# Part sums of finished accumulators spread over four units, and GpSimd's values made one group ahead, in a four-layer graph attention network

## What is computed

```python
h = x @ W                                   # per head
e = leaky_relu(s_src[i] + s_dst[j])         # slope 0.01 or 0.2
alpha = softmax(where(adj, e, -inf), axis=j)
out = alpha @ h                             # layer 0: then elu
```

## Time and profile before

| what | value |
| --- | --- |
| time, median of 3 runs | 3360.18 us (3354.19 to 3361.27) |
| time of the profiled execution | 3357.18 us |
| its span | 3355.4 us |
| busy, PE / DVE / ACT / POOL | 3011.8 / 2278.4 / 1914.1 / 1226.3 us |
| mean granted clock of PE | 0.961 |

### The profile page before, as it was taken

The page is one execution under the profiler, slowest core; times in us unless marked ns, Lnnn a source line. Parts: engine busy times, 40 slices in busy tenths (PEclk is TensorE's granted clock), DMA queues, the critical chain, the costliest instruction groups (busy, mean ns, idle before and its releaser), DMA issues.

```text
span 3355.4 us, 74122 instructions
## 1 busy us (share of the span) xinstructions
PE 3011.8 (90%) x26664; PEld 2751.1 (82%) x26664; DVE 2278.4 (68%) x4091; ACT 1914.1 (57%) x3380; POOL 1226.3 (37%) x1640
## 2 busy tenths in 40 slices
PE   6588899999955999999997999999999998569997
PEld 5587899999945999999995787887887886359997
DVE  4888788887777888888776555655655554454447
ACT  4455798889845898898884454444454443320000
POOL 2433456551214555545212013223223232324443
PEclk9799999999987999999998999999999998789999
DMA  7465000000100000000010000000000000000001
GB/s 258 177 243 205 10 13 11 12 13 13 61 0 11 13 13 11 12 13 10 12 40 7 9 2 4 4 1 4 4 1 4 1 1 2 0 1 0 0 0 50
DMA packets 42286, 104.58 MB, mean 31 GB/s; under 512 B 9904, under 2 KB 23472, under 8 KB 33968
## 3 DMA queue, kind: packets, MB, share of 16 engines
q1 hardware_dynamic: 42160, 102.92, 9.1%
HBM read 98.51 MB, written 4.39 MB: 31 GB/s over the span
## 4 chain that ended last, share of the span: by engine, by line
PE 73%; DVE 15%; issue 5%; DMA 3%; POOL 2%; ACT 1%; DVEq 1%; SPq 0%; POOLq 0%; ACTq 0%
PE bank L970 16%; PE bank L967 16%; PE bank L1014 14%; PE bank L1052 11%; PE bank L973 10%; DVE sums L1454 4%; DVE rings L1509 3%; PE bank L931 2%; DMA arena<-in_adj_dram 2%; DVE rings L1512 2%; PE bank L1041 2%; PE bank L1028 1%; PE bank L945 1%; DVE rings L1503 1%; DVE arena L1212 1%
## 5 line engine op out<-in xcount | busy, mean ns | idle before, releaser
L967 PE MATMUL bank<-values,rings 128*128 128x195 bf16 x8192 | 1418.4, 247 | 138.0 <-DVE rings L1512 79.0
L760 ACT ACTIVATE above<-srow,kpass 128x512 fp8e4<-128x512 f32 x2048 | 1292.9, 709 | 294.3 <-DVE rings L1512 278.6
L970 PE MATMUL bank<-values,rings 128*128 128x195 bf16 x8192 | 1418.6, 249 | 0.0
L967 PEld LDWEIGHTS bank<-values,rings 128*128 128x128 fp8e4 x8192 | 809.2, 99 | 157.2 <-issue 155.8
L970 PEld LDWEIGHTS bank<-values,rings 128*128 128x128 fp8e4 x8192 | 787.1, 96 | 1.1
L1509 DVE TENSOR_TENSOR rings<-rings,above 128x512 uint32<-128x512 uint32 x512 | 385.1, 752 | 237.2 <-PE bank L970 190.5
L778 ACT ACTIVATE values<-srow,cmul 128x512 f32<-128x512 f32 x256 | 205.9, 814 | 433.3 <-PE bank L1052 432.3
L1052 PE MATMUL bank<-hv,values 128*128 128x257 f32 x1792 | 423.8, 382 | 9.5 <-DVE values L1388 9.5
L1512 DVE TENSOR_TENSOR rings<-rings 128x512 uint32<-128x512 uint32 x512 | 408.6, 798 | 17.5
L1052 PEld LDWEIGHTS bank<-hv,values 128*128 128x128 f32 x1792 | 336.9, 191 | 80.5 <-issue 25.5
L973 PE MATMUL bank<-values,rings 128*128 128x195 bf16 x4096 | 349.3, 248 | 23.0 <-DVE rings L1500 23.0
(11 more groups left out here) (177 smaller groups left out, 3505.4 us busy)
## 6 DMA issues: line engine op xcount, KB each, us to landing
arena<-in_adj_dram SPq DMA_DIRECT2D x64, 1024.0 KB, 5.7
srow<-src_dram SPq DMA_DIRECT2D x72, 256.0 KB, 3.2
x<-in_x_dram SPq DMA_DIRECT2D x1, 4096.0 KB, 14.3
out_dram<-x SPq DMA_DIRECT2D x8, 512.0 KB, 2.9
arena<-in_L_gnn_fe_w_dram SPq DMA_DIRECT2D x2, 512.0 KB, 10.0
arena<-in_L_gnn_W_hz_dram SPq DMA_DIRECT2D x1, 1024.0 KB, 10.4
arena<-in_L_gnn_g_w_dram SPq DMA_DIRECT2D x1, 1024.0 KB, 11.6
weights<-in_L_gnn_W_dram SPq DMA_DIRECT2D x3, 256.0 KB, 3.3
```

The source lines that it names most:

```text
L760: last = act.activation(above[:, k % 2, q, :], srow[:, par, :], ACT.Relu, scale=BIG, bias=kpass[:, slot, q * BITS + k:q * BITS + k + 1], s ...
L967: pe.matmul(acc[:, 0:KW], pos[:, k % 2, q, :].bitcast(FP8)[:, rows], v[:, 0:KW], start=first, stop=final, skip_group_check=True)
L970: last = pe.matmul(acc[:, KW:2 * KW], neg[:, k % 2, q, :].bitcast(FP8)[:, rows], v[:, KW:2 * KW], start=False, stop=final, skip_group_chec ...
```

## The change

In layers 0 and 1, from the second pass of layer 0 on, the four part sums of a finished group are made one each in the units 1, 2, 3 and 4 of the group that follows, after the exclusive-or; the wait for banks and quotient stands ahead of the first, and `s_sums` is signalled by the last. The first pass of layer 0 (`at_once`) and layer 3 keep all four at once. On POOL, in every pass that makes values (three passes in each of layers 0, 1 and 3), the values of group 0 are made ahead of the loop, each trip makes the values of group g + 1 before the quotient of group g, and the last values and the last two quotients stand behind a loop of three double trips.

```diff
@@ -586,16 +586,33 @@
                     if p < H - 1:
 
                         pool.wait_ge(s_unit, p * UNITS + (CREDIT + TURN[l] * H * UNITS))
-                    with pool.Fori(0, NG // 2) as gg:
+                    if p == H - 1:
+                        with pool.Fori(0, NG // 2) as gg:
+                            for par in range(2):
+                                g = gg * 2 + par
+                                chain.enter(g, links)
+                                quotient(l, p, g, par)
+                        chain.leave(NG)
+                        continue
+
+                    def next_values(g):
+                        for kind in range(kinds):
+                            made = value_parts(pool, chain, vtmp_pool, kind, g * GT, GT, p + 1, 1 - p % 2)
+                        made.then_inc(s_vals, 1)
+
+                    next_values(0)
+                    chain.settle()
+                    with pool.Fori(0, NG // 2 - 1) as gg:
                         for par in range(2):
                             g = gg * 2 + par
                             chain.enter(g, links)
-                            if p < H - 1:
-                                for kind in range(kinds):
-                                    made = value_parts(pool, chain, vtmp_pool, kind, g * GT, GT, p + 1, 1 - p % 2)
-                                made.then_inc(s_vals, 1)
+                            next_values(g + 1)
                             quotient(l, p, g, par)
-                    chain.leave(NG)
+                    chain.leave(NG - 2)
+                    next_values(NG - 1)
+                    quotient(l, p, NG - 2, 0)
+                    quotient(l, p, NG - 1, 1)
+                    chain.settle()
                 if l < 3:
                     return
 
@@ -1442,16 +1459,23 @@
                 chain.leave(FIRST_CHUNKS)
                 rest_of_first_values(l)
 
+            def sum_parts(l, half, slot, it):
+
+                kinds = 2 if l < 3 else 1
+                parts = bank[GT * half + it][:, 0:kinds * KW].rearrange("p (k a c) -> p k c a", k=kinds, a=PARTS)
+                return dve.tensor_reduce(sums[:, slot, it, 0:kinds, :], parts, AX.X, ALU.add)
+
+            def banks_ready(l, count):
+
+                dve.wait_ge(s_unit, count * BITS + (TURN[l] * H * UNITS + CREDIT))
+
+                dve.wait_ge(s_quot, count + (TURN[l] * H * NG + CREDIT - 1))
+
             def evacuate(l, half, slot, count):
 
-                kinds = 2 if l < 3 else 1
-
-                dve.wait_ge(s_unit, count * BITS + (TURN[l] * H * UNITS + CREDIT))
-
-                dve.wait_ge(s_quot, count + (TURN[l] * H * NG + CREDIT - 1))
+                banks_ready(l, count)
                 for it in range(GT):
-                    parts = bank[GT * half + it][:, 0:kinds * KW].rearrange("p (k a c) -> p k c a", k=kinds, a=PARTS)
-                    last = dve.tensor_reduce(sums[:, slot, it, 0:kinds, :], parts, AX.X, ALU.add)
+                    last = sum_parts(l, half, slot, it)
                 last.then_inc(s_sums, 1)
 
             LINKS = {0: 2 * BITS, 1: 2 * BITS, 3: 0}
@@ -1482,7 +1506,7 @@
                         dve.tensor_scalar(xt, xt, lnst[:, i, 6:7], lnst[:, i, 9:10], ALU.subtract, ALU.mult)\
                             .then_inc(s_xmade, 1)
 
-            def group(l, g, gg, par, banks_before, packing=None, norm=None):
+            def group(l, g, gg, par, banks_before, packing=None, norm=None, at_once=False):
 
 
                 if norm is None:
@@ -1511,8 +1535,15 @@
                         dve.wait_ge(s_dve, chain.next())
                         dve.tensor_tensor(neg[:, r], edge[:, r], pos[:, r], ALU.bitwise_xor).then_inc(s_sides, 1)
 
-                    if k == (1 if packing is None else 0) and banks_before is not None:
-                        evacuate(l, banks_before, 1 - par, g)
+                    if l == 3 or at_once:
+                        if k == (1 if packing is None else 0) and banks_before is not None:
+                            evacuate(l, banks_before, 1 - par, g)
+                    elif 1 <= k <= GT and banks_before is not None:
+                        if k == 1:
+                            banks_ready(l, g)
+                        summed = sum_parts(l, banks_before, 1 - par, k - 1)
+                        if k == GT:
+                            summed.then_inc(s_sums, 1)
                     if packing is not None and k % 2 == 0:
                         convert(packing + k // 2)
                     if packing is not None and k % 2 == 1:
@@ -1532,7 +1563,8 @@
                         with dve.Fori(begin, end) as gg:
                             for par in range(2):
                                 group(0, gg * 2 + par, gg, par, 0,
-                                      gg * (2 * GT) + (PACKED_FIRST + par * GT) if begin == 0 else None)
+                                      gg * (2 * GT) + (PACKED_FIRST + par * GT) if begin == 0 else None,
+                                      at_once=True)
                     evacuate(0, 0, 1, NG)
                     group(0, NG, 0, 0, None)
                     group(0, NG + 1, 0, 1, 0)
```

More of the change, by code:

```diff
@@ L1443, in stats, with evacuate @@
                 rest_of_first_values(l)
-            def evacuate(l, half, slot, count):
+            def sum_parts(l, half, slot, it):
                 kinds = 2 if l < 3 else 1
+                parts = bank[GT * half + it][:, 0:kinds * KW].rearrange("p (k a c) -> p k c a", k=kinds, a=PARTS)
+                return dve.tensor_reduce(sums[:, slot, it, 0:kinds, :], parts, AX.X, ALU.add)
+            def banks_ready(l, count):
                 dve.wait_ge(s_unit, count * BITS + (TURN[l] * H * UNITS + CREDIT))
                 dve.wait_ge(s_quot, count + (TURN[l] * H * NG + CREDIT - 1))
+            def evacuate(l, half, slot, count):
+                banks_ready(l, count)
                 for it in range(GT):
-                    parts = bank[GT * half + it][:, 0:kinds * KW].rearrange("p (k a c) -> p k c a", k=kinds, a=PARTS)
-                    last = dve.tensor_reduce(sums[:, slot, it, 0:kinds, :], parts, AX.X, ALU.add)
+                    last = sum_parts(l, half, slot, it)
                 last.then_inc(s_sums, 1)
```

## The result

| | before | after |
| --- | --- | --- |
| median time, us | 3358.14 (4 runs, 3354.19 to 3361.27) | 3320.58 (4 runs, 3318.61 to 3322.90) |
| ratio, with its 95% interval | | 0.9889 (0.9872 to 0.9906) |
| profiled execution: time / span, us | 3357.18 / 3355.4 | 3322.40 / 3320.6 |

What follows compares the result with a forecast made beforehand. PE, busy 90% of the span, bounds the kernel; only its 53 stops behind DVE can be gained. 3357.18 - 36.6 + 1.2 = 3321.8, or 3324.8 from the median; forecast between them 3323 us, range 3315 to 3341.

Steps and rivals of the forecast that it cites:

- The stop and its count: Attention of layers 0 and 1: PE loses 0.69 us in each of 53 groups; spreading the sums saves 36.6 us.
- 5.87 - 1.42: DVE's time to PE's unit 2 start, less three moved sums: 4.45 us, under the 5.18 PE has work for.
- Unit 1 beside POOL: With every operation slowed before POOL's end, DVE's stretch from unit 1 into unit 2 takes 5.00 us, still under 5.18.
- rival 1: POOL blocks DVE once more in unit 1: stops of 0.5 to 0.7 in 38 groups, 3341 us; chance 0.11.
- the even durations of the sums: Part sums' durations spread by only 15 ns, read as agreeing that a tensor_reduce never contends with POOL.
- Pass starts: Second group, POOL beside units 1 to 4: a 0.15 to 0.6 us stop in three passes, 1.2 us given back.
- 3.8 after PE wants them: Without POOL one group ahead, a pass's last values would be ready 25.6 us after the last group began, 3.8 late.
- Rival 2: Units 1 to 4 with a part last over about 3.1 us, giving up to four stops a group: 3384; chance 0.04.
- Rival 3: The sums were not what is late; ACT or a hand-over takes their place, each stop stays: 3357; chance 0.05.
- The packing pass: Same POOL order except the second group's values, made under POOL's idle time: no change, at most 1 us either way.

Runs made afterwards that it cites:

- e5: Kernel before with all four sums still lumped in unit 1 and POOL's order as before, but POOL signalled one unit later: 3330.43 us, ratio 0.9922.
- e4: Changed kernel with three part sums in unit 1 and one in unit 2, POOL's order as before the change: 3321.57 us, ratio 0.9898.
- e9: The changed kernel itself measured again, against the kernel before: 3322.92 us, ratio 0.9901.
- e1: Changed kernel with part sums spread over units 1 to 4 but POOL's loop as before the change: 3346.0 us, ratio 0.9969.
- e6: Changed kernel with every part sum of units 1 to 4 made twice, the extra result unread: 3353.94 us, ratio 0.9998.
- e7: Changed kernel with every part sum of units 1 to 4 made three times, the extra results unread: 3455.65 us, ratio 1.0294.
- e10: Changed kernel with two part sums in each of units 1 and 2, POOL's order as before, second measurement: 3316.90 us, ratio 0.9879.
- e2: Kernel before with only POOL's order changed to one group ahead, all four sums still lumped in unit 1: 3358.8 us, ratio 1.0005.
- e3: Changed kernel with two part sums in unit 1 and two in unit 2, POOL's order as before the change: 3318.11 us, ratio 0.9882.

## Why the prediction was right

- **The stop and its count.** 53 stops of 0.69 were read; the two stretches gave 0.67 and 0.68 for each. 35.9 us came from them, 36.6 less 1.2 were expected. In the span 34.8 came, as the packing pass was 1.9 longer and two other stretches 0.9 shorter.
- **Its cause.** The chain was right, the share of the lump was not told apart: "5.87 - 1.42" took the lump as what must shrink. e5 shows that 0.48 of the 0.69 was POOL's contention in unit 2. The forecast did not suffer, since 5.87 - 1.42 is under 5.18 with the contention still in it, and the change removes both. For a part change it mattered: e4's sum by length alone, 3332, was wrong by 10 us, and the branch that counted POOL, 3321, was right.
- **Unit 1 beside POOL.** The dearest sum was 5.00 against 5.18. The trace has 2.69 to 2.86 from "and" to "and" in unit 1 (leaving out the group with PE's pause), where the dearest terms (0.90 + 0.92 + 0.47 + 1.15) give 3.44. In most groups beside values the "and" takes 0.69 and the exclusive-or 0.77 there, and the "and" of unit 2 still waits 0.42 for PE. Matmul gaps in the changed kernel are at most 0.04 longer than usual there, so rival 1 has fallen. The rule behind it, in the Trainium skill (SBUF — State Buffer, "Who interferes with whom"), that when VectorE and GpSimd want their shared port pair the loser waits for the other's whole instruction, is not contradicted: a single "and" takes up to 1.18 in place of 0.69, more than the 0.90 that the prediction called dearest, and in some units 0 the edge (0.88), the "and" (1.17) and the exclusive-or (1.14) are all long, as from 540.36. But those units have no sum; their three operations are 1.4 us longer together, and unit 1's never more than 0.8.
- **A reading that could not bear its weight.** The prediction took the even durations of the sums in the earlier trace rows as agreement that POOL does not slow them. In the kernel before POOL is idle during the lumps, so they could not show it. The changed kernel does: the sum at 546.36 lies beside POOL's operation at 546.04 and takes 0.55, as the others do 0.56.
- **Pass starts.** Expected was 0.4 in each of three, 1.2 in all. There are two: 0.24 us in layer 0's third pass, shown here, and 0.10 in layer 1's third pass (1429.73 to 1429.91), none in layer 1's second; e9, the same kernel, has the same two. Both stand where they were forecast, at the start of unit 5 of the second group; that they cost 0.3 and not 1.2 is a term sized too high:

```profile
601.40 0.25 PE L987 MATMUL bank<-values,rings 128*128 128x195 bf16 x1
601.73 0.24 PE L984 MATMUL bank<-values,rings 128*128 128x195 bf16 x1
```

- **POOL ahead.** "3.8 after PE wants them" was exact for POOL's end in e1, but by luck: 10.8 + 14.8 stood for 10.6 + 15.0. Then 0.67 of hand-over came on top. The forecast never priced its absence; e1 makes it 25 us.
- **Rival 2** asks for 3.1 us a unit. e6 with 2.9 to 3.1 stands at the time of before, e7 with about 3.35 far above it. So its point of decision was somewhat too lenient: DVE's limit is the sum over a group, and it lies nearer than the units suggest.
- **Rival 3** fell: ACT still waits for DVE, and the stops are gone.
- **The packing pass.** +1.9 us in this pair of traces, where "nothing, at most 1 either way" was forecast; that is inside the scatter named under e10, and its cause is open.

## What to carry to other kernels

When a lump of work on a helping engine stops the main one, read also what the end of the lump sets off: here the lump released the work of a third engine at the worst place, and a signal sent one unit later took away 0.48 of the 0.69 us. Spreading work delays its last part by as much as it is spread, so look for who waits for that part at the next boundary; the least spread that fits, here two units, needs nothing else moved. And measure the room that is left by adding known work in doses: take two doses, and read each kind of group by itself. Here both gave 1.6 us in groups without values, while those beside values had 1.1 and 1.3.

## What the runs showed that I had not expected

In ten of the twelve profiles PE pauses once for 2.9 to 3.4 us in layer 1's attention, between its second and third pass, without waiting for any engine (the view calls it issue); in e1 and e2 the view has another wait at that place. It is where PE's outer loop, whose body holds two passes, begins its second round. In seven of the ten, about 1 us behind the pause some 20 matmuls run at half their pace, 0.16 us apart, with a granted clock of about 0.50, the lower level of 1.2 GHz; in e3, e5 and e6, after pauses of the same length, the clock stays at 1.00, so this alone lets two executions differ by 1.6 us. The changed kernel, around it (busy us of PE, PEld, DVE, ACT, POOL, then the granted clock):

```profile
1388.00:1392.60 4.60, 1.37 (x17) 1.14 (x14) 2.70 (x6) 4.60 (x8) 0.00 (x0) 1.00 0.04 7
1392.60:1396.90 4.30, 4.22 (x31) 3.97 (x32) 0.00 (x0) 1.47 (x3) 0.00 (x0) 0.60 0.02 4
1397.00:1401.00 4.00, 4.00 (x50) 4.00 (x48) 3.12 (x6) 2.18 (x4) 0.00 (x0) 1.00 0.00 0
```

The middle row begins before the clock falls and so shows 0.60. Pause and slow matmuls cost this kernel some 5 us once (3.5 and 1.6). The cause of the pause was not looked for.
